# A new order of the steps in the attention loop: probability products in pairs of key tiles at most

## The reference

```python
qh = _split_heads(q @ wq_w.T + wq_b)
kh = _split_heads(k @ wk_w.T + wk_b)
vh = _split_heads(v @ wv_w.T + wv_b)
scores = jnp.einsum('bhqd,bhkd->bhqk', qh, kh) / jnp.sqrt(jnp.float32(D_K))
attn = jax.nn.softmax(jnp.where(mask, scores, -1e9), axis=-1)
out = jnp.einsum('bhqk,bhkd->bhqd', attn, vh)
```

## Time and profile before

| | |
|---|---|
| median of 3 runs | 1577.74 us (1574.93 to 1578.54) |
| the profiled execution | 1581.58 us, its span 1579.8 us |
| PE matmuls busy | 1487.5 us, 94% of the span |
| VectorE, ScalarE, GpSimd busy | 63%, 58%, 27% |
| granted TensorE clock, mean | 0.98 of full |
| bytes moved by DMA | 156.28 MB, mean 99 GB/s |

### The profile page before, as it was taken

The page is one execution under the profiler, slowest core; times in us unless marked ns, Lnnn a source line. Parts: engine busy times, 40 slices in busy tenths (PEclk is TensorE's granted clock), DMA queues, the critical chain, the costliest instruction groups (busy, mean ns, idle before and its releaser), DMA issues. The chain is left out here.

```text
span 1579.8 us, 56667 instructions
## 1 busy us (share of the span) xinstructions
PE 1487.5 (94%) x23708; PEld 1264.8 (80%) x23708; DVE 1002.9 (63%) x3974; ACT 917.8 (58%) x1836; POOL 424.8 (27%) x549
## 2 busy tenths in 40 slices
PE   6699999999999999999999999999999978886997
PEld 2578888888888888888888888888888844544997
DVE  4666677677666676767667667766666635442642
ACT  3346666665566665666556666665666644764653
POOL 0033333333333333333333333333333003002420
PEclk9899999999999999999999999999999998998999
DMA  5444444444444444444444444444444222000201
GB/s 150 139 121 109 109 109 109 109 109 109 112 119 121 127 113 106 117 112 121 110 116 114 116 113 117 116 110 110 109 109 109 68 86 85 2 1 8 61 21 54
DMA packets 89856, 156.28 MB, mean 99 GB/s; under 512 B 44784, under 2 KB 53744, under 8 KB 89328
## 3 DMA queue, kind: packets, MB, share of 16 engines
q1 hardware_dynamic: 89312, 151.56, 36.1%
q0 software_dynamic: 288, 1.05, 0.2%
HBM read 69.61 MB, written 4.19 MB: 47 GB/s over the span
## 5 line engine op out<-in xcount | busy, mean ns | idle before, releaser
L663 DVE CUSTOM_DVE_ANT_0 junk<-bank,mask_q 128x400 bf16<-128x400 f32 (+1 forms) x1024 | 546.9, 571 | 186.5 <-issue 180.3
L615 ACT ACTIVATE probs<-bank 128x512 f32<-128x512 f32 (+1 forms) x832 | 467.3, 595 | 123.2 <-PE bank L788 113.9
L591 POOL CAST ctx_hi<-ctx_raw 128x400 fp32r<-128x400 f32 x248 | 121.6, 519 | 847.8 <-PE bank L752 847.8
L788 PE MATMUL bank<-qstack,kstack 104*128 104x128 f16 (+1 forms) x3328 | 290.2, 220 | 4.2 <-ACT probs L615 3.4
L752 PE MATMUL bank<-wv_hi,ctx_hi 128*128 128x256 f32 (+1 forms) x832 | 280.1, 337 | 0.0
L769 PE MATMUL bank<-kstack,qstack 96*128 96x400 f16 (+1 forms) x1024 | 268.2, 336 | 7.4 <-issue 3.8
L654 DVE SCALAR_TENSOR_TENSOR k_lo<-bank,bk,k_hi 128x400 f16<-128x400 f32 (+1 forms) x256 | 162.2, 634 | 168.0 <-ACT k_hi L625 168.0
L635 ACT ACTIVATE v<-bank 128x256 f32<-128x256 f32 (+1 forms) x416 | 159.2, 383 | 188.5 <-PE bank L752 182.1
L788 PEld LDWEIGHTS bank<-qstack,kstack 104*128 104x128 f16 (+1 forms) x3328 | 214.2, 99 | 65.1 <-issue 16.7
L625 ACT ACTIVATE k_hi<-bank,bk 128x400 f16<-128x400 f32 (+1 forms) x256 | 152.1, 594 | 180.4 <-PE bank L742 172.3
L594 POOL TENSOR_TENSOR ctx_lo<-ctx_raw,ctx_hi 128x400 fp32r<-128x400 f32 x248 | 253.2, 1040 | 0.0
(11 more groups left out here) (169 smaller groups left out, 1727.2 us busy)
## 6 DMA issues: line engine op xcount, KB each, us to landing
ctx_raw<-in_ctxT SPq DMA_DIRECT2D x32, 1602.0 KB, 7.0
kstack<-k_hi SPq DMA_DIRECT2D x512, 100.1 KB, 2.2
kstack<-k_lo SPq DMA_DIRECT2D x256, 100.1 KB, 2.2
weight<-in_w SPq DMA_DIRECT2D x18, 256.0 KB, 2.7
x<-in_xT SPq DMA_DIRECT2D x8, 512.0 KB, 5.9
qstack<-q_parts SPq DMA_DIRECT2D x192, 16.0 KB, 5.6
out_yT<-x SPq DMA_DIRECT2D x1, 2048.0 KB, 6.4
weight<-in_sw SPq DMA_DIRECT2D x3, 512.0 KB, 6.6
```

Source lines behind the costliest of these rows:

```text
L591: nc.gpsimd.tensor_copy(c_hi[:, k, s0:s0 + n], raw[:, k, s0:s0 + n]).then_inc(ctx_hi, 1)
L615: nc.scalar.activation(probs[kt % NP][0:m, GROUPS * h:GROUPS * (h + 1), :], st[h][0:m, :], ACT.Exp, scale=DK ** -0.5 / (UP * UP)).then_inc ...
L663: nc.vector.tensor_tensor_reduce(junk[i % SM][:, 0:n], sm[i % SM][:, 0:n], w["mask_q"][:, s0:s0 + n], 1.0, -3.0e38, ALU.add, ALU.max, part ...
L788: mm = nc.tensor.matmul(st[h][0:m, g * PW:(g + 1) * PW], kstack[b.slot][0:KROWS, p, kt * P:kt * P + m], qstack[b.slot][0:KROWS, p, :], sta ...
```

## The change

The table `SLOTS` is replaced. Each step stands in it as often as before, and the functions behind the steps are the same.

```diff
-    SLOTS = ["L K K S0 S1", "K K O S0 S1 K K", "S0 S1 K K M M M", "S0 S1 V P P P P M V M M M", "V S0 S1 M V",
...
+    SLOTS = ["K K L S0 S1 K", "K S0 S1 K K O", "S0 S1 K K", "M S0 S1 M P P M V M M M V", "S0 S1 M M M V M P",
...
```

More of the change, by code:

```diff
@@ L504, in cross_attention @@
     QSTACK_DMAS = 6
-    SLOTS = ["L K K S0 S1", "K K O S0 S1 K K", "S0 S1 K K M M M", "S0 S1 V P P P P M V M M M", "V S0 S1 M V",
-             "M M M V S0 M S1 M", "M V H S0 M V M M S1", "V M S0 S1 H M P P P M", "M H M S0 V S1 M", "V S0 M M M S1",
-             "V S0 M M M S1 P", "P M S0 V M M S1 G H", "S0 V S1 T P N P P"]
+    SLOTS = ["K K L S0 S1 K", "K S0 S1 K K O", "S0 S1 K K", "M S0 S1 M P P M V M M M V", "S0 S1 M M M V M P",
+             "P M S0 S1 V M M H M V", "M V S0 S1 V P P M M", "S0 V M S1 M M P H P H", "S0 M M S1",
+             "V M M V S0 M M S1 V", "M S0 M M S1 P", "P M M S0 S1 M V", "H G V T S0 P P S1 N"]
     slots, counts = [], {}
```

## The result

The changed kernel takes 1594.53 us (median of 4 runs, 1592.23 to 1596.95) against 1577.34 us for the kernel before (median of 4, 1574.93 to 1578.54): 1.0111 times before, 95% interval 1.0091 to 1.0131, slower by some 17 us (14 to 21). The profiled execution has a span of 1593.7 us, 13.9 us over the one in the earlier trace rows.

A forecast was written before the change was run, and what follows sets the result against it. PE's own instruction stream was taken to bound the turns. Terms +28.5 - 7.4 - 3 + 4 - 11 = +11.1 us on the profiled 1581.6 gave 1592.7, less 3.8 for the median: 1588.8 us, range 1577 to 1600 us.

The forecast's parts named there:

- The price of a run: Each run of products on PE costs 0.23 us beyond its products; four more runs a turn, +28.5 us.
- K2's wait: Key chunk K2 waits for k_lo of K0; with L standing between, 0.17 us less a turn.
- K6's wait: Key chunk K6 is held by VectorE doing join O; with O moved later, 0.07 us less a turn.
- The waits of M8 and P7: New waits: M8 for M5's maximum, P7 for S15's exponential; 0.065 us each, +4 us together.
- The joints: Small differences where other steps meet in a turn: -0.1 us a turn, -3 us, between -5 and +2.
- The stalls: Instruction-supply stalls in runs of four products and key chunks behind L nearly all go: -11 us, bounds 0 and -13.
- M0's waits: M0 waits 3.8 us in all for keys copied after k_lo of K3; left unchanged, +6 us as other end.
- both readings: Stalls in PE's products come from dense runs and go, or from packet boundaries or DMA and stay: 1600 us, chance 0.10.

The follow-up runs named there:

- the last experiment: The changed kernel run unchanged once more, a single execution for a second profile: 1599.1 us.
- single products: The changed kernel with all six pairs of products broken up by a neighbouring step, 14 runs a turn instead of 8: 1634.79 us, 1.0382 of before.
- L apart: The kernel before with step L moved behind K0 and K1 instead of in front of them: 1570.33 us, 0.9967 of before.
- the two splits: The kernel before with P0 to P3 split into two pairs: by M3 alone 1586.11 us, 1.0067; by M3 and V1 1583.98 us, 1.0029.

## Why the prediction was right, and where its sum was short

The direction and the range held; the sum gave +11.1 us, and it was 17.2. By its steps:

- **The price of a run** was right: 0.23 us whatever its length. It gave 28.5 us for four more runs. Three of products and L at 0.23 us, and T apart at 0.28 to 0.30 us, are 30 to 31 us. The Trainium skill says under Key Properties of TensorEngine Tiling (Array Packing) that a change of the tiling mode drains the engine. The trace agrees in so far as 0.09 to 0.12 us fall on the way from a full tile to a narrow one and 0.11 to 0.17 us on the way back; that the engine drains in this time no row shows.
- **K2's wait** went as said (0.17 us, 5 us in all). **K6's wait** didn't: 0.50 before, 0.49 after. I had put it down to the join O on VectorE, and O moved away without effect. What is late is k_lo of K4: ScalarE begins k_hi of K4 0.12 us after the matmuls end, of K5 to K7 0.04 us, because K4's step has waits for copies of the stacked keys besides. That is read from the trace and wasn't tried by itself. 2 us of gain less than forecast.
- **The waits of M8 and P7** came to 0.07 and 0.06 us a turn (0.065 each forecast). **The joints** are what is left over in the median turn, about -2 us (-3 forecast).
- **The stalls** went, all of them: 13 to 14 us in turns 1 to 30, where I took 11. (The 0.014 us a record by which I worked out the loss is 0.45 us for the 32 records of a product; 1.93 us for 128 would be 0.015. It doesn't change the term.) M0's waits, which I left alone, were also 2 us smaller.
- These terms add up to some +12 us in the turns, close to the 11.1 of the sum, and that is in part luck: runs, K6 and the joints came out 5 us dearer than I had them, the stalls and M0's waits 4 to 5 us cheaper. Measured in the turns it is +11.9 us between the first profiles and +14.4 between the second ones, 13.2 on average.
- **What failed is what the sum left out: the last turn.** I counted turns up to the last T and took nothing for the stretch behind it. From the last T to the end of the products it is 22.0 us in both profiles of before and 26.4 and 26.3 us in both of the changed kernel: +4.3 us. Of this, 1.4 us stand in front of the turn's first scores, 1.0 us of it the wait of L for the exponential of S25. The other 3 us lie in the turn, where PE has no projections and waits for exponentials in both kernels. There P7 and the last L wait anew, but with the waits of the scores PE idles only 0.3 us more. Most of it goes with the 6.8 us at the lower clock, 2.4 us by the estimate of the last experiment's forecast. With the 4.3 us the sum is 15.4 us.

13.2 + 4.3 = 17.5 us lies next to the measured 17.2, but not all of the profiles is in it: their spans differ by 20.2 us on average, since what follows the loop took 292.5 and 290.5 us before and 291.0 and 298.6 us after. No code was changed there.

Whether the new waits cause the lower clock stays open. In the five profiled executions in which L waits in front of that turn (0.77 us in four, 0.19 us with single products), part of the turn was at the lower clock each time (3.4 to 10.2 us); of the six in which it doesn't wait, in two (3.4 us each). That fits, but the clock also fell elsewhere, inside the turns of some executions of a kernel and at other places in others.

Is it the narrow tile that costs? Products and T have another thing in common: they are the only plain fp32 matmuls of a turn, which the trace shows as two records each, while keys and values are fp32r and scores fp16. No run changed the width alone. But behind the loop, in the kernel before, plain fp32 (L1198, two matmuls) stands between fp32r (L1240, L1241), all with full tiles:

```profile
1317.51 1.88 PE L1198 MATMUL bank<-x,mean_w 128*128 128x512 f32 x4
1318.82 0.80 PE L1240 MATMUL bank<-rows,sel_a 128*128 128x512 f32 x1
1319.45 0.40 PE L1241 MATMUL bank<-rows,sel_b 128*128 128x512 f32 x1
```

The five records take 1.94 us from 1317.51 to 1319.45. A record of plain fp32 starts every 0.43 us in longer rows of this size and one of fp32r takes 0.22, which makes 1.94: nothing is left for the change of type.

What causes the stalls can be told from more than closeness, since the traces say where they fall. Take PE's instructions in order (weight loads, matmuls and the steps of its sequencer) and count. Five profiles have stalls with over 0.1 us of idle time, 36 in all: both of before, L apart, and the two splits. Every one of them stands at the same place in a block of 256 instructions, to within one. The first five of before, for example, are 4608, 5120, 1791 and 5121 instructions apart, multiples of 256 to within one, and moving a step doesn't move the place. The packets of the queue for instructions have 16 KB each, and there are 191 of them where the trace's count makes 189 blocks. Every one of the 36 stalls ends 1.2 to 1.6 us after such a packet has landed.

Density decides which block ends in a stall: the 256 instructions ahead of one took 2.2 to 3.4 us, where a block takes 7 us on average, and in the changed kernel none took under 3.4 us. So both readings held a part, the end of a packet giving the place and the dense stretch the loss. A few blocks as dense did not stall, and no run took a fetch away by itself.

## What to carry to other kernels

Count how often TensorE changes between matmuls with narrow weight tiles and full ones, not how many of each it has: a change there and back cost 0.23 us here, in a turn of 38 us, and nothing hid it, since PE was the bound. Join such work into runs, but not so long that it asks for instructions faster than they come: where no run was over three there were no stalls, four lost up to 2 us in a turn now and then. An order that is tuned for the steady turns must be looked at in the last one too, where its cover is gone.

## What the runs showed that I had not expected

A single small matmul step (T, 8 columns, once a turn, two records) costs 0.4 us between full tiles and 0.12 us inside a run of narrow ones. Stalls of PE for instructions also come when the dense stretch is broken by 0.27 us, and they fall in the same turns: 2, 14 and 26 for L in all four profiles that have them, and each of 5, 10, 17 and 29 for P3 in four of five. That is a period of 12 turns, which are 16640 instructions of PE, 65 blocks of 256. A step of PE that waits for two semaphores (K2, M8, P7, L) starts 0.14 to 0.15 us after the last thing it needs, one with a single semaphore (K6, scores) after 0.05 us. And two executions of one kernel differed by some 3 us each ahead of the loop, in turn 0 and behind the loop (up to 7.6 us there), so a single profile is a poor base for a sum of a few microseconds; its median turn, which repeats to 0.01 us, is a good one.
